# Mixer of a two-layer model: the eighth chunk's intra product goes to the state product's bank, and the second conv tile's first steps go ahead of output-weight splits

## The chip, the cores and the metric

One core of a Trainium2 chip runs the whole program. The metric is the time of one execution on the device in microseconds (us), the median over several executions. The core has a matrix engine (PE, with its weight loads shown apart as PEld), a vector engine (DVE), an activation engine (ACT), a GpSimd engine (POOL) and a queue that only starts transfers (SP). Each works through its own list in order; they meet only at semaphores. PE writes into PSUM, which has eight banks of 128 x 512 floats.

## The reference

The program computes `x = x + f(layernorm(x))` four times on a 1024 x 512 matrix: a state-space mixer, a gated feed-forward with 4-bit weights, a small attention over heads, and a feed-forward with routed low-rank parts. Only the first, the mixer, is touched:

```
proj = x_norm @ in_proj_w.T             # gate 4096, conv channels 4096+1024+1024, dt 64
xBC  = silu(conv4(proj_hbc))            # causal, 4 taps along time
x, B, C = split(xBC);  dt = softplus(dt + dt_bias);  dA = exp(-dt * exp(A_log))
state = state * dA_t + (dt*x)_t * B_t   # per head (64 heads, 8 groups), over 1024 steps
y_t   = state . C_t ;  y = y + x * D
yn    = y * rsqrt(mean(y*y over the group) + eps) * norm_weight * silu(gate)
out   = yn @ out_proj_w.T               # added to x
```

## The kernel before

The mixer runs over 8 groups `g` (8 heads, 512 channels each) and in each over 8 chunks `c` of 128 time steps; `n = 8*g + c`. Group 0 and group 7 are written out, groups 1 to 6 are one hardware loop (five jumps back). All matrix products with 512 columns on weights are made in three passes from a high and a low part (`three_pass`, L69 to 89). A group's input weights are 10 tiles (6 conv tiles and 4 of the gate), its output weights 4 tiles (numbers 10 to 13). A weight tile is loaded by SP into a ring of four, ACT makes the high part (`w_round`, L434 and L437), DVE or POOL the low part (`w_rest`, L595 and L597 on DVE, L408 on POOL): this is a split.

The scan is written in chunk form. In each chunk PE does, in this order (L868 to L930): transposes of x into bank `p_x` (L878); the transposes of the z of the chunk before into `p_in` (L838); B transposed and B.C into `p_gb` (L885, L886); the decay exponents into `p_d0` and `p_d1` (L894); a conv tile for a later half (`conv_tile`, L84 and L88) or else the next chunk's gate product; the output product of the chunk before into `p_y` (`out_product`); the state read (inter product, `p_in`, L910); the new state's part (state product, `p_x`, L916; not in the eighth chunk); in chunks 0, 1, 4 and 5 a second conv tile into `p_d1`; the product inside the chunk (intra product, L927, 16 pieces of 64 columns) into `p_y`; and, where a conv tile was made, the next chunk's gate product (`p_gate`).

On DVE a chunk has: B.C masked (L653) and copied (L654), the low part of z (L579), the decays times B.C (`em`, L661), splits, a conv tile's taps (`tile_taps`, L559, L563, L567), the residual `x_res += p_y * g_rstd` (L587), which is the reader of the output product, y from the inter product (L685), the state (L692 or L695), the y sum with the intra product (L704, in chunk 0 L709), and `z = y * gate` (L713). Between the L685 and L704 steps POOL adds `x_d` to y (L391). DVE begins each group with five small copies (L640, L642). On ACT a conv tile is taken out of its bank by `tile_in` (L445), which DVE's first tap waits for (`s_cin`), and finished by `tile_silu` (L450), which waits for the taps (`s_tap`).

Two places are touched. First, the intra product of every chunk waits for the residual of the chunk before (`s_res`), as both use `p_y`; the transposes of x of a group's first chunk wait only for ACT's copy out of `p_x` in the chunk before (`s_xs`). Second, in chunk 0 of each group ACT makes the high parts of output weights 10 and 11 and then calls `tile_in` of conv tile 1, and DVE makes their low parts and then the tile's first tap; the tile's other taps come after z, and chunk 1's decay product (L894) waits until all are done, because tile 1 lies in `p_d1`.

Of the kernel before, what the change touches and what calls it, by code (L numbers as in the profile page):

```python
# [19 lines left out]
ALU = mybir.AluOpType  # L20
# [3 lines left out]
P = 128  # L24
# [4 lines left out]
NC = L // P  # L29
# [4 lines left out]
HD = 64  # L34
# [57 lines left out]
def mixer(nc, io, ctx, x_res, ident, mean_var2, rstd2, q_prep):  # L92
# [30 lines left out]
    em = sb("em", [P, 2, HG * P])  # L123
# [75 lines left out]
    def tapped(g, hf, j):  # L199

        return (g * 2 + hf) * TILES * TAPPED[0] + (g * TILES + hf * j) * (TAPPED[1] - TAPPED[0]) + j * TAPPED[0]

    def bank_of(j):

# [222 lines left out]
    @block.scalar  # L427
    def _(act):
        def w_round(g, w):

            n = g * WT + w
            act.wait_ge(s_raw[w % RAW], 16 * (g * len(range(w % RAW, WT, RAW)) + w // RAW + 1))
            if w < TILES + KT:
                act.activation(w_hi[:, w, :], w_raw[:, w % RAW, :], ACT.Copy).then_inc(s_whi, 1)  # L434
            else:
                k = w - TILES - KT
                act.activation(w_hi[:, w, :], w_raw[:, w % RAW, :], ACT.Copy, scale=norm_w[:, bass.ds(g, 1), k])\  # L437
                    .then_inc(s_whi, 1)

        def tile_in(T, g, j, bank=None):  # L440

            p = bank_of(j) if bank is None else bank
            act.wait_ge(s_prj, T + 1)
            wait(act, s_xc, T - 1)
            act.activation(conv[:, j % 2, :], p[:], ACT.Identity, bias=conv_w[:, bass.ds(g, 1), j, TAPS],  # L445
                           scale=conv_w[:, bass.ds(g, 1), j, TAPS - 1]).then_inc(s_cin, 1)

        def tile_silu(T, g, j, hf):
            act.wait_ge(s_tap, tapped(g, hf, j) + TAPPED[hf])
            act.activation(xbc[:, j, half_cols(hf)], conv[:, j % 2, :], ACT.Silu).then_inc(s_xc, 1)  # L450

        def z_round(m):
            act.wait_ge(s_zt, m + 1)
            act.activation(zt_hi[:].rearrange("p k t -> p (k t)"), p_in[:], ACT.Copy).then_inc(s_zhi, 1)  # L454

        def gate_silu(m):

            act.wait_ge(s_gate, m + 1)
            wait(act, s_z, m)
            act.activation(gate[:], p_gate[:], ACT.Silu).then_inc(s_sg, 1)  # L460

        def group(g, last):
            for c in range(NC):
                n = g * NC + c
                first = isinstance(g, int) and n == 0
                left, now, later = conv_tiles(g, last, c)
                splits = () if last else SPLIT_IN.get(c, ())
                for tile in left:
                    tile_silu(*tile)
                act.wait_ge(s_xt, n + 1)  # L470
                wait(act, s_xd, n - 1)
                act.activation(xs[:, c % 2, :], p_x[:], ACT.Copy).then_inc(s_xs, 1)  # L472
                if not first:
                    z_round(n - 1)
                act.wait_ge(s_d, n + 1)
                wait(act, s_intra, n - 1)
                for k, p in enumerate((p_d0, p_d1)):
                    act.activation(em[:, c % 2, k * 512:(k + 1) * 512], p[:], ACT.Exp).then_inc(s_e, 1)  # L478
                for T, tg, j, _ in now:
                    tile_in(T, tg, j)  # L480
                if c == NC - 1 and not last:
                    act.wait_ge(s_gate, n + 1)
                for w in splits:
                    w_round(g + 1, w)
                for tile in now:
                    tile_silu(*tile)
                if c == 0:
                    wait(act, s_out, n)
                    w_round(g, TILES + KT)
                    w_round(g, TILES + KT + 1)  # L490
                for T, tg, j, _ in later:
                    tile_in(T, tg, j)
                act.wait_ge(s_y, n + 1)
                wait(act, s_ss, n)
                wait(act, s_v, n - 1)
                act.activation(junk[:], y[:, c % 2, :], ACT.Square, accum_out=ss[:, c % 2:c % 2 + 1])\  # L496
                    .then_inc(s_ss, 1)
                if not (last and c == NC - 1):
                    gate_silu(n + 1)
                if c == 0:  # L500
                    w_round(g, TILES + KT + 2)
                    w_round(g, TILES + KT + 3)


        for c in range(NC):
            act.wait_ge(ln_tr, c + 1)
            act.activation(xn_hi[:, :, c * P:(c + 1) * P], (p_x, p_in)[c % 2][:].rearrange("p (k t) -> p k t", k=KT),
                           ACT.Copy).then_inc(ln_hi, 1)
            if c >= CH:
                w_round(0, c - CH)  # L510
        act.wait_ge(s_const, 16 * 6)

        act.wait_ge(dt_ve, 4)
        act.activation(t_e, t_v, ACT.Abs).then_inc(dt_ac, 1)
        act.wait_ge(dt_ac, 1)
        act.activation(t_e, t_e, ACT.Exp, scale=-1.0).then_inc(dt_ac, 1)
        act.activation(head_c[:, 3:4], head_c[:, 1:2], ACT.Exp).then_inc(dt_ac, 1)
        act.wait_ge(dt_ve, 5)
        act.activation(t_r, t_w, ACT.Ln).then_inc(dt_ac, 1)
        act.wait_ge(dt_ac, 4)  # L520
        act.activation(t_rem, t_r, ACT.Exp, scale=-1.0).then_inc(dt_ac, 1)
        w_round(0, 4)
        w_round(0, 5)
        tile_in(0, 0, 0, p_tile)
        tile_in(1, 0, 1, p_d1)
        for w in range(TILES, TILES + KT):
            w_round(0, w)

        act.wait_ge(dt_tp, 4)
        act.activation(by_half(ecum_t), transposed(p_y), ACT.Exp).then_inc(dt_ac, 1)  # L530
        act.activation(by_half(dtw_t), transposed(p_gb), ACT.Exp).then_inc(dt_ac, 1)
        act.activation(by_half(etot_t), transposed(p_d0), ACT.Exp).then_inc(dt_ac, 1)
        for j in range(TILES):
            tile_silu(j, 0, j, 0)
            if j + 2 < TILES:
                tile_in(j + 2, 0, j + 2, (p_tile, p_d1)[j % 2])
        gate_silu(0)
        group(0, False)
        with act.Fori(1, G - 1) as g:
            group(g, False)  # L540
        group(G - 1, True)
        z_round(LAST)

    @block.vector
    def _(ve):
# [89 lines left out]
        def group(g, last):  # L635
# [7 lines left out]
            for c in range(NC):  # L643
# [43 lines left out]
                if c < NC - 1:  # L687
                    ve.wait_ge(s_stn, st + 1)
                    wait(ve, s_stu, st)
                    if c > 0:  # L690
                        ve.wait_ge(s_std, g * (NC - 2) + c)
                        ve.tensor_tensor(state[:], p_x[:], state_dec[:], ALU.add).then_inc(s_stu, 1)  # L692
                    else:
                        wait(ve, s_inter, st)
                        ve.tensor_copy(state[:], p_x[:]).then_inc(s_stu, 1)  # L695
                if c == 0:
                    w_rest(g, TILES + KT)
                    w_rest(g, TILES + KT + 1)
                for tile in later:
                    tile_taps(*tile, range(1))  # L700
                ve.wait_ge(s_intra, n + 1)
                if c > 0:
                    ve.wait_ge(s_txd, st)
                    ve.tensor_tensor(y[:, c % 2, :], y[:, c % 2, :], p_y[:], ALU.add).then_inc(s_y, 1)  # L704
                else:
                    ve.wait_ge(s_xd, n + 1)
                    wait(ve, s_ss, n - 1)
                    wait(ve, s_z, n - 1)
                    ve.tensor_tensor(y[:, c % 2, :], x_d[:], p_y[:], ALU.add).then_inc(s_y, 1)  # L709
# [109 lines left out]
    def _(pe):  # L819
# [36 lines left out]
                gate_product(n + 1, 0)  # L856

        def out_product(m):
            pe.wait_ge(s_zhi, m + 1)
            three_pass(pe, p_y[:], lambda k: (zt_hi[:, k, :], zt_lo[:, k, :]),  # L860
                       lambda k: (w_hi[:, TILES + KT + k, :], w_lo[:, TILES + KT + k, :]), GW // P,
                       lambda: pe.wait_ge(s_zlo, m + 1)).then_inc(s_out, 1)

        def group(g, last):
            for c in range(NC):
# [7 lines left out]
                if c > 0:  # L873
                    pe.wait_ge(s_stu, g * (NC - 1) + c)
                else:
                    wait(pe, s_xs, n)
                for j in range(GW // P):
                    mm = pe.transpose(p_x[:, j * P:(j + 1) * P], xbc[:, j, cs], ident[:])  # L878
                mm.then_inc(s_xt, 1)
# [42 lines left out]

                pe.wait_ge(s_m, 2 * (n + 1))
                pe.wait_ge(s_xdt, n + 1)
                wait(pe, s_res, n)
                for h in range(HG):
                    mm = pe.matmul(p_y[:, h * HD:(h + 1) * HD], em[:, c % 2, h * P:(h + 1) * P],  # L927
                                   x_dt[:, h * HD:(h + 1) * HD], start=True, stop=True)
                mm.then_inc(s_intra, 1)
                if now:  # L930
# [974 lines left out]
```

## Time and profile before

| | |
|---|---|
| median of 3 runs | 1380.57 us (1378.35 to 1381.72) |
| profiled execution, its own time | 1378.48 us |
| its span | 1376.7 us |
| PE busy | 1287.1 us (93%) |
| PE weight loads | 1008.3 us (73%) |
| DVE busy | 922.1 us (67%) |
| ACT busy | 676.4 us (49%) |
| POOL busy | 548.9 us (40%) |
| mean granted PE clock | 0.975 |

The profiled execution's time is 2.09 us below the median of the runs; its span is 1.8 us below its own time. The mixer's groups lie between about 66 and 1018 us of the span, and a middle group takes 119.4 us (one group's eighth intra product starts at 537.95 us, the next one's at 657.35 us). Timeline rows give the start and the busy time in us, then engine, line, operation, output and inputs, how many instructions are merged, and in brackets how long the engine sat idle before and what ended that. Ends of PE's instructions are modelled, so starts are the better measure.

### The profile page before, as it was taken

How to read it: one execution, taken by the hardware profiler on the slowest of the kernel's cores; microseconds unless marked ns; L12 is line 12 of the kernel's file. 1: busy time of each engine (PE TensorE's matmuls, PEld its weight loads, DVE VectorE, ACT ScalarE, POOL GpSimd, SP SyncE). 2: the span in 40 equal slices, each digit the busy share in tenths (PEclk: the TensorE clock that was granted, in tenths of full speed). 3: DMA queues.
4: the chain of work that ended last, by engine and by line, in shares of the span. 5: the costliest groups of instructions: out<-in, count | busy, mean ns of one | idle time of the engine just before them, and what ended most of it. 6: DMA issues, size and time to landing. Idle time of an engine off the chain costs nothing. (4 is left out here: it accounts for less than half of the span.)

```text
span 1376.7 us, 20683 instructions
## 1 busy us (share of the span) xinstructions
PE 1287.1 (93%) x6252; PEld 1008.3 (73%) x6262; DVE 922.1 (67%) x1756; ACT 676.4 (49%) x1055; POOL 548.9 (40%) x551
## 2 busy tenths in 40 slices
PE   5699999999999999999999999999869999879986
PEld 4577877877887887788788778778646766667764
DVE  5876677667667766766766676676656445368995
ACT  3465565566556556656655566655323223222220
POOL 2145345444533534443454354334333333333331
PEclk9899999999999999999999999999979999999997
DMA  4111011011102101100200120000013222131200
GB/s 150 59 48 33 1 56 40 17 32 47 31 1 63 31 16 32 55 23 1 71 23 16 32 62 16 3 30 2 8 42 115 85 76 80 50 99 29 58 16 23
DMA packets 44248, 57.61 MB, mean 42 GB/s; under 512 B 10182, under 2 KB 21156, under 8 KB 43922
## 3 DMA queue, kind: packets, MB, share of 16 engines
q1 hardware_dynamic: 44178, 56.84, 13.7%
q8 instruction: 23, 0.38, 0.1%
q14 instruction: 47, 0.39, 0.1%
HBM read 49.87 MB, written 6.96 MB: 41 GB/s over the span
## 5 line engine op out<-in xcount | busy, mean ns | idle before, releaser
L372 POOL TENSOR_TENSOR x_w<-xs,head_g 128x512 f32<-128x512 f32 x56 | 58.6, 1046 | 279.1 <-ACT xs L472 254.5
L559 DVE SCALAR_TENSOR_TENSOR conv<-p_tile,conv_taps,conv 128x511 f32<-128x511 f32 x189 | 140.9, 745 | 32.5 <-ACT conv L445 22.8
L927 PEld LDWEIGHTS p_y<-x_dt,em 128*128 128x128 f32 x1024 | 123.5, 192 | 32.9 <-issue 29.8
L391 POOL TENSOR_TENSOR y<-y,x_d 128x512 f32<-128x512 f32 x56 | 72.0, 1285 | 160.8 <-DVE y L685 160.8
L927 PE MATMUL p_y<-x_dt,em 128*128 128x64 f32 x1024 | 121.8, 272 | 11.4 <-DVE x_res L587 11.4
L661 DVE TENSOR_TENSOR em<-em,p_gb 128x512 f32<-128x512 f32 x128 | 82.2, 684 | 73.6 <-ACT em L478 73.6
L450 ACT ACTIVATE xbc<-conv 128x512 f32<-128x512 f32 x96 | 60.4, 630 | 130.1 <-DVE conv L567 73.6
L84 PE MATMUL p_tile<-xn_hi,w_hi 128*128 128x512 f32 x252 | 111.5, 443 | 2.9 <-DVE halo L563 2.9
L496 ACT ACTIVATE junk<-y 128x512 f32<-128x512 f32 x64 | 40.6, 635 | 142.3 <-DVE y L704 128.7
L559 DVE SCALAR_TENSOR_TENSOR conv<-p_d,conv_taps,conv 128x511 f32<-128x511 f32 (+2 forms) x99 | 73.8, 746 | 54.6 <-ACT conv L445 50.7
L84 PE MATMUL p_gate<-w_hi,xn_hi 128*128 128x512 f32 x256 | 106.2, 415 | 1.1 <-ACT gate L460 1.1
L408 POOL TENSOR_TENSOR w_lo<-w_raw,w_hi 128x512 fp32r<-128x512 f32 x64 | 83.1, 1314 | 59.1 <-ACT w_hi L434 59.1
L84 PE MATMUL p_y<-w_hi,zt_hi 128*128 128x512 f32 x256 | 102.5, 400 | 2.2 <-ACT zt_hi L454 2.2
L84 PE MATMUL p_y<-w_lo,zt_hi 128*128 128x512 f32 x256 | 102.4, 400 | 0.0
L84 PE MATMUL p_gate<-w_lo,xn_hi 128*128 128x512 f32 x256 | 100.3, 392 | 0.0
L84 PE MATMUL p_tile<-xn_lo,w_hi 128*128 128x512 f32 x252 | 99.3, 394 | 0.0
L478 ACT ACT_TABLE_LOAD x64 | 82.1, 1283 | 1.1
L375 POOL TENSOR_TENSOR x_dt<-xs,head_g 128x512 f32<-128x512 f32 x64 | 66.9, 1046 | 30.4 <-ACT xs L472 30.4
L450 ACT ACT_TABLE_LOAD x61 | 78.3, 1283 | 1.1
L88 PE MATMUL p_y<-w_hi,zt_lo 128*128 128x512 f32 x256 | 70.8, 399 | 0.0
L478 ACT ACTIVATE em<-p_d 128x512 f32<-128x512 f32 x128 | 69.6, 596 | 0.7
L1102 POOL TENSOR_TENSOR f_w_lo<-wf,f_w_hi 128x512 fp32r<-128x512 f32 x22 | 30.3, 1377 | 99.4 <-ACT f_w_hi L1143 99.4
(293 smaller groups left out, 3279.2 us busy)
## 6 DMA issues: line engine op xcount, KB each, us to landing
w_raw<-w SPq DMA_DIRECT2D x112, 256.0 KB, 2.8
q_words<-q SPq DMA_DIRECT2D x33, 256.0 KB, 2.7
h_ring<-h_lo_rows SPq DMA_DIRECT2D x6, 704.0 KB, 5.0
h_lo_rows<-h_rest SPq DMA_DIRECT2D x11, 256.0 KB, 2.0
x_res<-x SPq DMA_DIRECT2D x8, 256.0 KB, 4.6
out<-out_t SPq DMA_DIRECT2D x8, 256.0 KB, 2.2
h_lo_rows<-h_rest SPq DMA_DIRECT2D x11, 128.0 KB, 1.9
decay_lhs<-cum_parts SPq DMA_DIRECT2D x64, 6.0 KB
```

The source lines that it names most:

```text
L84: pe.matmul(out, lhs(k)[0], rhs(k)[n], start=(start and k == 0 and n == 0), stop=False)
L88: last = pe.matmul(out, lhs(k)[1], rhs(k)[0], start=False, stop=(k == k_tiles - 1))
L372: pool.tensor_tensor(by_head(x_w[:]), by_head(xs[:, c % 2, :]), heads(DTW, c), ALU.mult)\
L375: pool.tensor_tensor(by_head(x_dt[:]), by_head(xs[:, c % 2, :]), heads(DT, c), ALU.mult)\
L391: pool.tensor_tensor(y[:, c % 2, :], y[:, c % 2, :], x_d[:], ALU.add).then_inc(s_txd, 1)
L408: pool.tensor_tensor(w_lo[:, w, :], w_raw[:, w % RAW, :], w_hi[:, w, :].bitcast(F32), ALU.subtract)\
L450: act.activation(xbc[:, j, half_cols(hf)], conv[:, j % 2, :], ACT.Silu).then_inc(s_xc, 1)
L478: act.activation(em[:, c % 2, k * 512:(k + 1) * 512], p[:], ACT.Exp).then_inc(s_e, 1)
L496: act.activation(junk[:], y[:, c % 2, :], ACT.Square, accum_out=ss[:, c % 2:c % 2 + 1])\
L559: ve.scalar_tensor_tensor(out=conv[:, s, sh:], in0=p[:, 0:HALF - sh], scalar=conv_w[:, bass.ds(g, 1), j, tap], in1=conv[:, s, sh:], op0=AL ...
L661: ve.tensor_tensor(m, m, gm.unsqueeze(1).broadcast_to([P, HG // 2, P]), ALU.mult)\
L927: mm = pe.matmul(p_y[:, h * HD:(h + 1) * HD], em[:, c % 2, h * P:(h + 1) * P], x_dt[:, h * HD:(h + 1) * HD], start=True, stop=True)
```

## The change

The eighth chunk's intra product is written to `p_x` instead of `p_y`, and read from there by the y sum. It then waits for the chunk's own copy out of `p_x` (`s_xs`) and no longer for the residual. That wait is put ahead of each output product, and the first x transposes of a group wait for the y sum (`s_y`) of the chunk before. In chunk 0 `tile_in` and the first tap of conv tile 1 are written ahead of the splits of output weights 10 and 11, on ACT and on DVE.

```diff
+    def y_bank(c):
+        return p_x if c == NC - 1 else p_y
 # ACT, in group
+                for T, tg, j, _ in later:
+                    tile_in(T, tg, j)
                 if c == 0:
                     wait(act, s_out, n)
                     w_round(g, TILES + KT)
                     w_round(g, TILES + KT + 1)
-                for T, tg, j, _ in later:
-                    tile_in(T, tg, j)
                 act.wait_ge(s_y, n + 1)
 # DVE, in group
+                for tile in later:
+                    tile_taps(*tile, range(1))
                 if c == 0:
                     w_rest(g, TILES + KT)
                     w_rest(g, TILES + KT + 1)
-                for tile in later:
-                    tile_taps(*tile, range(1))
                 ve.wait_ge(s_intra, n + 1)
                 if c > 0:
                     ve.wait_ge(s_txd, st)
-                    ve.tensor_tensor(y[:, c % 2, :], y[:, c % 2, :], p_y[:], ALU.add).then_inc(s_y, 1)
+                    ve.tensor_tensor(y[:, c % 2, :], y[:, c % 2, :], y_bank(c)[:], ALU.add).then_inc(s_y, 1)
 # PE
         def out_product(m):
+            wait(pe, s_res, m)
             pe.wait_ge(s_zhi, m + 1)
 ...
                 if c > 0:
                     pe.wait_ge(s_stu, g * (NC - 1) + c)
                 else:
-                    wait(pe, s_xs, n)
+                    wait(pe, s_y, n)
 ...
-                wait(pe, s_res, n)
+                if c < NC - 1:
+                    wait(pe, s_res, n)
+                else:
+                    pe.wait_ge(s_xs, n + 1)
                 for h in range(HG):
-                    mm = pe.matmul(p_y[:, h * HD:(h + 1) * HD], em[:, c % 2, h * P:(h + 1) * P],
+                    mm = pe.matmul(y_bank(c)[:, h * HD:(h + 1) * HD], em[:, c % 2, h * P:(h + 1) * P],
                                    x_dt[:, h * HD:(h + 1) * HD], start=True, stop=True)
```

## Rows read from the trace of the kernel before

**Rows 1.** Waits, all engines: engine, line, releaser: us in total, times, longest us.

```profile
PE p_y L927 <- DVE x_res L587: 11.4, 9, 1.5
```

**Rows 2.** Groups by line: busy us, mean ns, idle before and its releaser.

```profile
L894 PE MATMUL p_d<-decay_rhs,decay_lhs 90*128 90x512 bf16 x128 | 38.3, 380 | 3.7 <-DVE conv L567 3.6
```

**Rows 3.** Windows: one middle group's eighth chunk; length, busy us by engine, PE clock.

```profile
530.04:543.06 13.02, 11.52 (x59) 9.13 (x59) 8.23 (x14) 8.16 (x13) 5.97 (x6) 1.00 0.25 83
```

**Rows 4.** Timeline of PE from a middle group's eighth intra product on.

```profile
537.95 1.97 PE L927 MATMUL p_y<-x_dt,em 128*128 128x64 f32 x16 [1.50 <-DVE x_res L587]
...
542.57 0.60 PE L878 MATMUL p_x<-identity,xbc 128*128 128x128 f32 x4
543.00 0.60 PE L838 MATMUL p_in<-identity,z 128*128 128x128 f32 x4
```

**Rows 5.** Timeline of DVE over the same group boundary.

```profile
540.83 0.69 DVE L704 TENSOR_TENSOR y<-y,p_y 128x512 f32<-128x512 f32 x1 [1.47 <-POOL y L391]
541.55 0.69 DVE L713 TENSOR_TENSOR z<-y,gate 128x512 f32<-128x512 f32 x1
544.68 0.20 DVE L640 TENSOR_SCALAR head_g<-dt_t 128x64 f32 x1 [2.44 <-issue]
...
546.46 1.28 DVE L661 TENSOR_TENSOR em<-em,p_gb 128x512 f32<-128x512 f32 x2
548.56 0.75 DVE L559 SCALAR_TENSOR_TENSOR conv<-p_tile,conv_taps,conv 128x511 f32<-128x511 f32 x1 [0.82 <-ACT conv L445]
```

**Rows 6.** Timeline of POOL in the eighth chunk and in the first chunk after.

```profile
535.38 2.57 POOL L408 TENSOR_TENSOR w_lo<-w_raw,w_hi 128x512 fp32r<-128x512 f32 x2 [3.22 <-ACT w_hi L434]
...
553.04 1.05 POOL L365 TENSOR_TENSOR state_dec<-state,head_g 128x512 f32<-128x512 f32 x1 [3.91 <-DVE state L695]
```

**Rows 7.** Timeline of PE, first chunk's second conv tile to the second chunk's decays.

```profile
552.44 1.07 PE L88 MATMUL p_d<-xn_hi,w_lo 128*128 128x512 f32 x4
553.35 1.89 PE L927 MATMUL p_y<-x_dt,em 128*128 128x64 f32 x16
...
559.65 0.61 PE L894 MATMUL p_d<-decay_rhs,decay_lhs 90*128 90x512 bf16 x2 [0.38 <-DVE conv L567]
```

**Rows 8.** Timeline of ACT in the same first chunk.

```profile
552.87 1.32 ACT L437 ACTIVATE w_hi<-w_raw,norm_scale 128x512 fp32r<-128x512 f32 x2
554.09 0.76 ACT L445 ACTIVATE conv<-p_d,conv_taps 128x512 f32<-128x512 f32 x1
```

**Rows 9.** Timeline of DVE in the same first chunk.

```profile
553.73 1.56 DVE L597 SCALAR_TENSOR_TENSOR w_lo<-w_raw,norm_scale,w_hi 128x512 fp32r<-128x512 f32 x2 [0.77 <-ACT w_hi L437]
555.22 0.74 DVE L559 SCALAR_TENSOR_TENSOR conv<-p_d,conv_taps,conv 128x511 f32<-128x511 f32 x1
555.88 0.67 DVE L709 TENSOR_TENSOR y<-x_d,p_y 128x512 f32<-128x512 f32 x1
...
558.86 0.73 DVE L567 SCALAR_TENSOR_TENSOR conv<-halo,conv_taps,conv 128x3 f32<-128x3 f32 x3
559.58 1.42 DVE L597 SCALAR_TENSOR_TENSOR w_lo<-w_raw,norm_scale,w_hi 128x512 fp32r<-128x512 f32 x2
```

**Rows 10.** Timeline, chunk 4: a conv tile passed on without splits between.

```profile
493.08 1.07 PE L88 MATMUL p_d<-xn_hi,w_lo 128*128 128x512 f32 x4
...
494.34 0.78 ACT L445 ACTIVATE conv<-p_d,conv_taps 128x512 f32<-128x512 f32 x1 [2.16 <-PE p_d L88]
495.35 0.75 DVE L559 SCALAR_TENSOR_TENSOR conv<-p_d,conv_taps,conv 128x511 f32<-128x511 f32 x1 [2.53 <-ACT conv L445]
```

**Rows 11.** Timeline of ACT and of DVE in group 0's first chunk.

```profile
75.69 1.32 ACT L437 ACTIVATE w_hi<-w_raw,norm_scale 128x512 fp32r<-128x512 f32 x2
...
78.64 0.67 DVE L709 TENSOR_TENSOR y<-x_d,p_y 128x512 f32<-128x512 f32 x1
```

**Rows 12.** Timeline of POOL and of DVE in the mixer's very last chunk.

```profile
1006.12 1.27 POOL L391 TENSOR_TENSOR y<-y,x_d 128x512 f32<-128x512 f32 x1 [3.32 <-DVE y L685]
...
1007.60 0.69 DVE L704 TENSOR_TENSOR y<-y,p_y 128x512 f32<-128x512 f32 x1 [1.55 <-PE p_y L927]
```

## The prediction

> **What bounds the kernel.** I read the waits first. Of everything that PE waits for inside the mixer's groups, two places belong to this change. The intra product (L927) waits for the residual 9 times, 11.4 us in all [rows 1]: once near the end of each of the eight groups, 1.25 us in group 0, 1.5 in each of groups 1 to 6, 0.96 in group 7, and once 0.16. The decay products (L894) wait for conv taps for 3.6 us in all [rows 2]: 1.31 in group 0 and about 0.38 in each of groups 1 to 6. Then the windows: in a middle group's eighth chunk PE is busy 11.52 of 13.02 us at full granted clock, and the 1.50 that are missing are that one wait [rows 3, 4]. So in the groups PE is the bound, with two holes per group (119.4 us), and the time of the mixer is PE's work plus those holes. Everything below asks how large each hole is afterwards, in one middle group (the one whose rows are shown); the rest of PE's list moves rigidly with it, and nothing later in a group has slack to give back or to absorb, since PE shows no other hole there.
>
> **Edit 1, the bank of the eighth intra product.** Removed: the wait for the residual, 1.50 us; the intra product would start 1.5 earlier, and its other conditions (em, x_dt, the copy out of p_x) are fulfilled long before. The gate product follows; it wants POOL's low parts of the gate weights, done at 535.38 + 2.57 = 537.95 [rows 6], while it could start at about 538.1: no hold. The x transposes after it would start at 542.57 - 1.5 = 541.07 [rows 4].
>
> What is late next: they now wait for the y sum (s_y). DVE's y sum starts at 540.83, released by POOL's add and not by the intra product, so it does not get earlier; it ends at 541.52 [rows 5]. From DVE's end to PE's start takes 0.06: the last tap ends at 558.86 + 0.73 = 559.59 and L894 starts at 559.65 [rows 9, 7]. So x transposes at 541.58. Behind the waiting transposes stand PE's z transposes, then the next group's whole list; for the x transposes wait ACT's copy and POOL's x_w, and as they come 1.0 earlier than before even so, those lose nothing. The z transposes come 0.43 after them (543.00 - 542.57), at 542.01, but z itself ends at 541.55 + 0.69 = 542.24 [rows 5], again unmoved: z transposes at 542.30. Before they were at 543.00. The hole of 1.50 therefore turns into one of about 0.8 further on, and the gain is 0.70. I take 0.05 off for a restart after idling: 0.65.
>
> Does it last? In the five jumps back DVE sits 2.44 us before its first small copy ("issue") after z, and z does not move, so DVE's chain stays where it is: em done at 546.46 + 1.28 = 547.74, then the first conv tap, which was at 548.56 because of ACT's tile_in [rows 5] and is asked for at 548.56 - 0.65 = 547.91. There is 0.17 left, so DVE doesn't bind. Seven boundaries: 7 x 0.65 = 4.5 us.
>
> Group 7 has no boundary behind it. There the y sum starts at 1007.60, released by PE, while POOL's add is done at 1006.12 + 1.27 = 1007.39 [rows 12]. Hardly anything to win: 0.1 us. The bounds for one boundary are 0 (below) and 1.5 (the whole hole); 0.65 stands on rows.
>
> The wait added ahead of each output product is for a residual of one chunk earlier, fulfilled long before. Whether a further fulfilled wait costs PE time: L927 stands behind three waits, and starts 0.91 after the four L88 products before it, which is four times 0.23, their pace [rows 7]. So it costs nothing; the bounds are 0 and, at 0.05 for each of some 60, 3 us.
>
> **Edit 2, the first chunk.** Before, in the middle group: ACT makes the two high parts from 552.87 on and tile_in at 554.09 [rows 8]; DVE makes the low parts from 553.73, the first tap at 555.22, the y sum at 555.88 [rows 9]. Both splits lay in time in which PE was still at the conv tile, so ACT and DVE would have idled.
>
> After: tile_in can start when PE has done the tile. In chunk 4, with nothing between, ACT starts 494.34 - 493.08 = 1.26 after the last four products start, and DVE's tap 1.01 after ACT [rows 10]. The last four start at 552.44 [rows 7], so ACT at 553.70 and the tap at 554.71: 0.51 earlier than 555.22. But the splits come behind: ACT's high parts start at about 554.40; the first low part was 0.86 after the first high part (553.73 - 552.87), so it is ready at 555.26, and the tap frees DVE after 0.66 (555.88 - 555.22) at 555.37. Two low parts without a wait take 1.42, 0.08 less to the next start [rows 9]: 1.34. The y sum comes at 556.71 to 556.75 instead of 555.88: later by 0.85; I take 0.87. The intra product, which it also waits for, is over by 553.35 + 1.89 = 555.24, so before and after the y sum waits for DVE's own list. Behind the y sum stand z, the other taps and the splits 12 and 13, with nothing that they could skip; the last tap ends at 560.46 and L894 starts at 560.52 instead of 559.65. PE's hole grows from 0.38 to about 1.25. The z transposes ahead of it do not matter, as L894 waits for the later taps anyway. ACT's silu of tile 1, the copies behind it and SP's loads of the next weights, which wait for splits 12 and 13, move by at most the same 0.87, as PE does. In sum, an idle stretch that was filled is now empty, and its work stands between the intra product and the taps.
>
> Group 0 is another case. ACT's high parts start at 75.69, behind tile 0's silu and not behind an early end of anything on PE [rows 11]. tile_in takes that place, the tap comes 1.01 later at 76.70, 0.66 + 1.34 on the y sum at 78.70, against 78.64: 0.06. Group 7 I count like a middle group. Sum: 7 x 0.87 + 0.06 = 6.1 us later.
>
> The bounds per group: if both splits were still hidden the tap's 0.51 would remain and the hole of 0.38 would close (-0.4); if tile_in's start takes 0.15 longer, or high part 11 holds DVE, +1.1.
>
> A rule of the Trainium skill bears on that. In the rows the first pair of low parts takes 1.56 and the later pair 1.42, and POOL's state_dec runs from 553.04 to 554.09, over the start of the first pair [rows 6, 9]. The page "SBUF — State Buffer", section "SBUF: two separate sides", says that GpSimd and a vector instruction with two SBUF inputs hold one pair of ports exclusively, the loser waiting in full. By that rule the moved pair, which starts after 554.09, takes 1.42, as I have put it; by a pair that always needed 1.56 the delay would be 1.0 per group and the sum 1 us more.
>
> **Sum.** -4.5 - 0.1 + 6.1 = +1.5 us. Against the profiled execution: span 1376.7 to 1378.2, own time 1378.48 to 1380.0. That execution was 2.09 below the median, so the median goes from 1380.57 to 1382.1.
>
> **Rivals.**
> A, the earlier first tap shortens the chain to L894: tile 1's taps end earlier and L894's wait goes, -3.6 us [rows 2], and with edit 1's 4.6 the time is 1372.4. For it: the tap is 0.5 earlier. Against: the splits are the same 1.3 us of DVE and now have no cover.
> B, edit 1 gives its whole hole, 7 x 1.5 = 10.5, less 6.1: 1376.2. That wants z 0.8 us earlier; its chain runs over POOL's add and DVE's list, none of which waits for the intra product.
> C, on the other side: the boundary gives nothing, and the splits' 6.1 remain: 1386.7. Place: the start of each group in the loop. If DVE's gap after z, 2.44 us here, depends on what PE does, or if the restart of PE behind two real waits in a row takes longer, DVE's chain of 3.06 us to the end of em (544.68 to 547.74) becomes the bound. It begins to eat at a gap of 2.6 and has eaten all at 3.3; from 0.3 of gain left per boundary downward the total passes 0.3%. For it: only 0.17 of slack. Against: the gap was measured with the same code.
> D, the edits cost beside this: the extra waits show with up to 3 us, or splits 12 and 13 now meet POOL's x_w: up to 1385, inside the range.
>
> **Chances.** Forecast 0.74 (own range 1379.5 to 1384.5), A 0.07, B 0.05, C 0.10, D 0.04. The range for 8 in 10 reaches from 1377.5, towards B, to 1386.5, towards C. A measurement here can't tell less than about 0.3% (4.1 us) from no change. A and part of B are faster by more: 0.11. C and a little of D are slower by more: 0.14. The rest, 0.75, is within.
>
> **What would show it.** Right: L927 in chunk 8 without idle; at the boundary the z transposes idle about 0.2 to 0.7 behind z, the x transposes about 0.5 behind y; a period of 119.4 + 0.2; DVE idle 1.7 before the first tap of tile 1, the y sum at once behind low part 11; L894's idle 1.25 in groups 1 to 7. Wrong: if L894's idle is 0.4 or less (A), if z transposes don't wait (B), if the taps of tile 0 follow em without idle time (C).

## The result and the profile after

| kernel | median us (lowest to highest, runs) | kernel before, beside it |
|---|---|---|
| changed kernel | 1382.88 (1380.26 to 1386.07, 20) | 1379.07 (1377.46 to 1384.91, 20) |

The ratio is 1.0021, with a 95% interval of 1.0013 to 1.003: 2.9 us slower, 1.8 to 4.1. Here and below, a difference in us without further words is this ratio, less one, times the median of the kernel before; the two medians themselves lie 3.8 apart. The 2.9 are inside the 0.3% that I had called no change, but clear of zero. I had forecast +1.5 us, and 1382.1. The absolute time came out only 0.8 off, and that is luck: the median of three runs from which I started, 1380.57, was 1.5 above the one of twenty runs, and this hid as much of an error of 2.3 in the difference of the medians. The profiled execution has a span of 1379.2 us, against 1376.7.

First the waits of PE over the mixer in the changed kernel (columns as in [rows 1]):

```profile
PE p_d L899 <- DVE conv L571: 10.0, 8, 1.3
PE p_in L842 <- DVE z L717: 5.9, 5, 2.5
PE p_x L883 <- DVE y L708: 3.6, 7, 0.6
```

L899 was L894, L842 was L838, L883 was L878. The 11.4 us behind the residual [rows 1] are gone down to one wait of 0.2; the new 3.6 at the x transposes stand at seven boundaries; and the decay products wait 10.0 instead of 3.6 [rows 2]. The 5.9 for z are a wait of 0.16 in group 0 and four in the last group, the longest of them, 2.5, at the z of the last chunk, which was 1.5 before. Then PE's timeline of the same middle group (start, busy time, operation, idle time before):

```profile
538.33 1.89 PE L935 MATMUL p_x<-x_dt,em 128*128 128x64 f32 x16
...
543.61 0.66 PE L883 MATMUL p_x<-identity,xbc 128*128 128x128 f32 x4 [0.55 <-DVE y L708]
544.34 0.66 PE L842 MATMUL p_in<-identity,z 128*128 128x128 f32 x4
...
553.83 1.07 PE L88 MATMUL p_d<-xn_hi,w_lo 128*128 128x512 f32 x4
554.74 1.89 PE L935 MATMUL p_y<-x_dt,em 128*128 128x64 f32 x16
...
561.96 0.60 PE L899 MATMUL p_d<-decay_rhs,decay_lhs 90*128 90x512 bf16 x2 [1.30 <-DVE conv L571]
```

The eighth intra product (L935) now has no idle time [rows 4], and the second hole has grown from 0.38 [rows 7] to 1.30. DVE over the same stretch:

```profile
542.87 0.69 DVE L708 TENSOR_TENSOR y<-y,p_x 128x512 f32<-128x512 f32 x1 [1.47 <-POOL y L395]
543.59 0.69 DVE L717 TENSOR_TENSOR z<-y,gate 128x512 f32<-128x512 f32 x1
546.96 0.20 DVE L644 TENSOR_SCALAR head_g<-dt_t 128x64 f32 x1 [2.67 <-issue]
...
548.74 1.27 DVE L665 TENSOR_TENSOR em<-em,p_gb 128x512 f32<-128x512 f32 x2
549.95 0.75 DVE L563 SCALAR_TENSOR_TENSOR conv<-p_tile,conv_taps,conv 128x511 f32<-128x511 f32 x1
...
556.19 0.75 DVE L563 SCALAR_TENSOR_TENSOR conv<-p_d,conv_taps,conv 128x511 f32<-128x511 f32 x1 [1.84 <-ACT conv L449]
556.86 1.41 DVE L601 SCALAR_TENSOR_TENSOR w_lo<-w_raw,norm_scale,w_hi 128x512 fp32r<-128x512 f32 x2
558.18 0.68 DVE L713 TENSOR_TENSOR y<-x_d,p_y 128x512 f32<-128x512 f32 x1
...
561.17 0.73 DVE L571 SCALAR_TENSOR_TENSOR conv<-halo,conv_taps,conv 128x3 f32<-128x3 f32 x3
```

and ACT and POOL in the first chunk:

```profile
555.08 0.78 ACT L449 ACTIVATE conv<-p_d,conv_taps 128x512 f32<-128x512 f32 x1 [0.73 <-PE p_d L88]
555.75 1.32 ACT L441 ACTIVATE w_hi<-w_raw,norm_scale 128x512 fp32r<-128x512 f32 x2
```

```profile
554.42 1.04 POOL L369 TENSOR_TENSOR state_dec<-state,head_g 128x512 f32<-128x512 f32 x1 [3.03 <-DVE state L699]
```

**Where the 2.9 us are.** I count from chunk to chunk on PE, by the start of the decay products of chunk 1. In the middle groups before they come at 320.83, 440.25, 559.65, a period of 119.40; after at 322.63, 442.29, 561.96, a period of 119.67. So a group costs 0.27 more, where I had 0.22: +0.92 in chunk 1 (the hole, 1.30 for 0.38) and -0.66 at the boundary. From group 0's first B transpose to these products of group 6 it is 731.00 us in the trace of before and 732.38 after (798.45 - 67.45; 801.29 - 68.91): +1.4. Further executions, told of below, give 731.02 and 731.03 for before and 732.38, 732.41 and 732.43 for after, so this much is the edits, and it is firm. What lies ahead of the first B transpose belongs to no edit and varies (67.45, 68.08, 67.72 before; 68.91, 68.80, 67.67, 68.71 after). The rest arises behind it: from the first B transpose to the first product of the next phase before has 952.36, 952.52 and 952.25, after 953.58, 954.69, 954.08 and 956.33, and the mean is 2.3 longer (954.67 against 952.38). Of this later. The 0.6 that are left of 2.9 (2.9 - 2.3) lie within the interval.

### The profile page after: what moved, and what is told of

Read it like the earlier page. It is cut to its first block and busy times, and to the rows that moved or that the text cites. A ratio compares the mean times of both kernels' runs of the same rounds, so it can differ in the third digit from the quotient of the medians.

```text
span 1379.2 us, 20756 instructions
## 1 busy us (share of the span) xinstructions
PE 1289.3 (93%) x6262; PEld 1008.8 (73%) x6262; DVE 919.9 (67%) x1756; ACT 677.7 (49%) x1055; POOL 549.0 (40%) x551
## 5 line engine op out<-in xcount | busy, mean ns | idle before, releaser
L935 PEld LDWEIGHTS p_y<-x_dt,em 128*128 128x128 f32 x896 | 108.6, 192 | 15.3 <-issue 12.2
L935 PE MATMUL p_y<-x_dt,em 128*128 128x64 f32 x896 | 106.1, 271 | 0.2 <-DVE x_res L591 0.2
```

The costliest lines, as they stand in the source:

```text
L935: mm = pe.matmul(y_bank(c)[:, h * HD:(h + 1) * HD], em[:, c % 2, h * P:(h + 1) * P], x_dt[:, h * HD:(h + 1) * HD], start=True, stop=True)
```

## The experiments

Each kernel was timed beside the kernel before, on the same chip. There were two sets: each edit alone, the splits last and the wait alone (kernel before: 1379.14, 23 runs), and the rest (1379.39, 23 runs).

### Each edit alone

**Edit 1 alone.** The changed kernel with the order of before on ACT and DVE:

```diff
+                if c == 0:
+                    wait(act, s_out, n)
+                    w_round(g, TILES + KT)
+                    w_round(g, TILES + KT + 1)
                 for T, tg, j, _ in later:
                     tile_in(T, tg, j)
...
+                if c == 0:
+                    w_rest(g, TILES + KT)
+                    w_rest(g, TILES + KT + 1)
                 for tile in later:
                     tile_taps(*tile, range(1))
```

> The kernel before with the bank edit alone (eighth intra product in p_x, its waits), ACT's and DVE's order in the first chunk as before. Theory of the prediction: each of seven group boundaries wins 0.65 us, bound by z, the tail 0.1, so 4.6 us less than before; the hole before the decay products of chunk 1 stays at 0.38 (1.31 in group 0). Rival C: the boundary wins nothing, time as before. Rival B: the whole hole of 1.5 us goes, 10.5 us less.

Measured: 1375.22, ratio 0.9966 [0.9951, 0.9981], 4.7 us faster; I had 4.6. The period is 118.73, which is 0.67 less. Its waits:

```profile
PE p_x L883 <- DVE y L708: 3.7, 7, 0.6
PE p_d L899 <- DVE conv L571: 3.5, 7, 1.3
```

A wait of 1.50 was taken away, and 0.67 of it was gained.

**Edit 2 alone.** The kernel before with the order of the changed kernel:

```diff
                 for T, tg, j, _ in later:
                     tile_in(T, tg, j)
                 if c == 0:
                     wait(act, s_out, n)
                     w_round(g, TILES + KT)
                     w_round(g, TILES + KT + 1)
...
                 for tile in later:
                     tile_taps(*tile, range(1))
                 if c == 0:
                     w_rest(g, TILES + KT)
                     w_rest(g, TILES + KT + 1)
```

> The kernel before with the reordering alone (tile_in and first tap of conv tile 1 ahead of splits 10 and 11 on ACT and DVE). Theory of the prediction: the splits lose the cover of the conv tile; the decay products of chunk 1 wait 0.87 to 0.92 us longer in groups 1 to 6 and about as much in group 7, nothing in group 0: 6 us more than before. Rival A: the earlier tap closes the hole of 0.38 per group, 3.6 us less.

Measured: 1391.66, ratio 1.0077 [1.0058, 1.0097], 10.6 us slower, against 6.1. So the edits do not add: -4.7 and +10.6 make +5.9, together they cost 2.9. The list of waits explains only the forecast part, 6.4 us more at L894 (10.0 for 3.6):

```profile
PE p_y L927 <- DVE x_res L587: 10.4, 8, 1.5
PE p_d L894 <- DVE conv L567: 10.0, 8, 1.3
```

The starts of L894 show it: 202.07, 322.40, 444.31, 564.63, 686.55, 806.90, 928.35. The steps are 119.9 into group 1 and then 120.3 (119.40 + 0.93, as forecast) and, every second time, 121.9, or 121.45 into group 7. Windows of this kernel (length, busy time of PE, PEld, DVE, ACT, POOL, granted clock, DMA share, GB/s), at the boundary into group 2, which was not lengthened, and at the one into group 3, which was:

```profile
299.00:302.00 3.00, 2.23 (x18) 2.23 (x19) 2.13 (x4) 0.63 (x1) 1.51 (x2) 1.00 0.87 280
...
420.00:424.00 4.00, 3.90 (x21) 3.55 (x22) 2.46 (x5) 0.95 (x2) 1.36 (x2) 0.70 0.47 165
424.00:426.00 2.00, 2.00 (x8) 1.64 (x7) 0.37 (x1) 0.41 (x2) 0.00 (x0) 0.74 0.01 4
```

and PE at the second:

```profile
420.10 2.27 PE L927 MATMUL p_y<-x_dt,em 128*128 128x64 f32 x16 [1.50 <-DVE x_res L587]
422.13 0.78 PE L84 MATMUL p_gate<-w_hi,xn_hi 128*128 128x512 f32 x1
```

PE stood idle for 1.50 us, and in the next microseconds the granted clock was 0.70 and 0.74 on the mean, between the upper level of 2.4 GHz and the lower of 1.2. The intra product took 2.27 us where it takes 1.97 [rows 4]. Each such place costs 1.6 us. The three long steps make 4.7 us, and 6.1 + 4.7 is 10.8: the trace has the same 10.8 up to the decay products of group 7 (860.94 from the first B transpose, for 850.16), and 10.6 are measured. In the kernel before the same idle of 1.50 is there in the same groups, and its clock over 418 to 422 us is 1.00. With edit 1 the 1.50 is gone, and the clock stays up at these places. So edit 1 is worth more beside edit 2 than alone: 7.7 us (10.6 - 2.9) for 4.7 by the measured times, 9.3 for 4.8 in the traces up to group 7. I had no rival for this.

Why the clock falls here and not in the kernel before is not shown. What is new is the hole of 1.30 in each group, but it does not stand beside the fall: the last one before it is 98 us earlier (322.40) and the next comes only at 443. It also changes when the boundaries come, every 120.3 us and no longer every 119.40. No run that keeps the 1.50 has the one without the other.

### Is the added wait ahead of the output products free?

```diff
         def out_product(m):
+            wait(pe, s_res, m)
             pe.wait_ge(s_zhi, m + 1)
```

> The kernel before with nothing but the wait for the residual of one chunk earlier added ahead of each output product (63 waits that are always fulfilled). Theory of the prediction: 0 us. Rival D: a fulfilled wait costs PE up to 0.05 us each, 3 us more, which would be the part of the measured 2.9 us that the groups' rows do not show.

Measured, the kernel before with that line alone: 1379.81, ratio 0.9999 [0.9984, 1.0015], and a period of 119.40 as in the kernel before. Free, as forecast; the 3 us of rival D are refuted.

### What bounds the boundary, y or z?

Edit 1 alone, but the eighth intra product in `p_d1`, so that the x transposes needn't wait for the y sum:

```diff
     def y_bank(c):
-        return p_x if c == NC - 1 else p_y
+        return p_d1 if c == NC - 1 else p_y
...
-                    wait(pe, s_y, n)
+                    wait(pe, s_xs, n)
```

> As e1_bank_only, but the eighth intra product goes to the bank p_d1, so the x transposes of the next group wait for nothing of the y sum (as in the kernel before). Theory: the hole at the boundary is set by z, which the z transposes need, and the wait of the x transposes costs nothing by itself: period as in e1_bank_only, 118.74 us, with PE's idle now all before the z transposes. Rival: the new wait for the y sum is what is left of the hole; without it 0.55 us less per boundary, 3.8 us in all.

Measured: 1376.79, ratio 0.9975 [0.9962, 0.9988], 3.4 us faster, and the same period as with edit 1 alone (118.73 to 118.78 for 118.72 to 118.74). PE's timeline shows the whole remainder in front of the z transposes:

```profile
539.39 0.60 PE L883 MATMUL p_x<-identity,xbc 128*128 128x128 f32 x4
540.82 0.66 PE L842 MATMUL p_in<-identity,z 128*128 128x128 f32 x4 [0.83 <-DVE z L717]
```

The two kernels were timed in different sets; their intervals overlap, and the periods are equal. So the wait for y in edit 1 costs nothing of its own; z is what the boundary waits for, as I had worked out.

### What the moved splits cost, and where they fit

**Splits last.** The changed kernel with the two low parts behind the tile's taps:

```diff
                 for tile in later:
                     tile_taps(*tile, range(1))
-                if c == 0:
-                    w_rest(g, TILES + KT)
-                    w_rest(g, TILES + KT + 1)
...
                 if c == 0:
+                    w_rest(g, TILES + KT)
+                    w_rest(g, TILES + KT + 1)
                     w_rest(g, TILES + KT + 2)
                     w_rest(g, TILES + KT + 3)
```

> The changed kernel, but DVE's low parts of output weights 10 and 11 moved behind all taps of conv tile 1, in front of those of 12 and 13. Theory: what costs in the reordering is the place of the two low parts between first tap and y sum, not the early tile_in; without them the y sum comes 0.5 us earlier than in the kernel before, the hole ahead of the decay products closes in groups 1 to 7 and mostly in group 0 (together 4.8 us), beside the 4.6 of the bank: 9.4 us less than before. Rival: four low parts in a row make DVE late in chunk 1 (output product waits for low part 13, or em comes late) and the hole only moves: about as e1_bank_only, 4.6 less, or worse.

Measured: 1374.13, ratio 0.9948 [0.993, 0.9967], 7.2 us faster than before. From DVE and from PE:

```profile
554.92 3.53 DVE L601 SCALAR_TENSOR_TENSOR w_lo<-w_raw,norm_scale,w_hi 128x512 fp32r<-128x512 f32 x4
```

The fourth of these low parts by itself, and POOL beside it:

```profile
556.91 1.53 DVE L601 SCALAR_TENSOR_TENSOR w_lo<-w_raw,norm_scale,w_hi 128x512 fp32r<-128x512 f32 x1
```

```profile
556.73 1.17 POOL L376 TENSOR_TENSOR x_w<-xs,head_g 128x512 f32<-128x512 f32 x1 [6.89 <-ACT xs L476]
```

```profile
554.97 0.61 PE L898 MATMUL p_d<-decay_rhs,decay_lhs 90*128 90x512 bf16 x2
...
557.25 1.07 PE L88 MATMUL p_tile<-xn_hi,w_lo 128*128 128x512 f32 x4
558.50 0.50 PE L84 MATMUL p_y<-w_hi,zt_hi 128*128 128x512 f32 x1 [0.18 <-DVE w_lo L601]
```

The decay products have no idle time in any group but the first (0.37, for 1.31 before). The splits are therefore the whole of what holds L894, and the sooner tap is worth nothing beside them. But the period is 118.77, not the 118.4 that the closed hole should give: the fourth low part now ends at 558.45, and the output product behind it starts at 558.50, where the four products before it, 0.91 after their start, would have let it start at 558.16. A hole of 0.38 was closed and one of 0.34 opened; PE's row shows only 0.18 of it as idle, and the other 0.08 of the period I can't place. The fourth low part is late not because four are too many: it takes 1.53 where the others take 0.75, as it starts behind POOL's `x_w` (556.73 to 557.90). With 0.75 it would have ended at 557.7, ahead of 558.16. In group 7 the fourth one starts ahead of POOL, all four take 2.73, and it is POOL's `x_w` that takes 1.45. Beyond edit 1's 4.6 this kernel gains 1.5 in group 0 (13.45 us from the first B transpose to the decay products, for 14.94); the 1.1 that are left of the 7.2 I can't place, and the interval is some 2.6 wide to either side. Of my 9.4 the part that failed is the hole that only moved, which was the rival.

**One split early, one late.** On ACT and DVE split 10 goes ahead of the tile's first steps; ACT makes high part 11 behind `tile_in`, DVE its low part at the end:

```diff
                 if c == 0:
                     w_rest(g, TILES + KT)
-                    w_rest(g, TILES + KT + 1)
                 for tile in later:
                     tile_taps(*tile, range(1))
...
                 if c == 0:
+                    w_rest(g, TILES + KT + 1)
                     w_rest(g, TILES + KT + 2)
                     w_rest(g, TILES + KT + 3)
```

> The changed kernel with split 10 back ahead of tile_in and first tap, and split 11 behind: high part after tile_in on ACT, low part behind all taps on DVE. In e3_splits_last the hole before the decay products closed, but PE then waited 0.18 (0.5 by the period, 118.75) for low part 13 before the output product of chunk 1. Theory: DVE idles 1.8 us before the first tap, room for one low part; with one less behind the taps low part 13 is no longer late: period about 118.2 us, 9 us less than before in all. Rival: split 10 still delays tile_in or the tap on ACT or DVE, or low part 13 stays late: as e3_splits_last, 7 less.

Measured: 1372.70, ratio 0.9941 [0.9922, 0.9959], 8.1 us faster; I had 9. The period is 118.35 (437.66 to 556.01): 0.67 less by edit 1 and 0.38 less by the hole. 7 x 1.05 and 0.7 in group 0 make the 8.1. DVE shows why it fits: one split fills the idle time ahead of the tap, and three at the end are done at 558.01.

```profile
550.48 0.90 DVE L602 SCALAR_TENSOR_TENSOR w_lo<-w_raw,norm_scale,w_hi 128x512 fp32r<-128x512 f32 x1 [0.77 <-ACT w_hi L441]
551.57 0.75 DVE L564 SCALAR_TENSOR_TENSOR conv<-p_d,conv_taps,conv 128x511 f32<-128x511 f32 x1 [0.19 <-issue]
...
555.94 2.07 DVE L602 SCALAR_TENSOR_TENSOR w_lo<-w_raw,norm_scale,w_hi 128x512 fp32r<-128x512 f32 x3
```

**And y's first step ahead of the residual.** What is left is z. POOL's add waits for DVE's L685 step, which stands behind the residual and a tap. In the eighth chunk the residual needn't come first any more, since the intra product no longer waits for it:

```diff
+                def y_inter():
+                    ...
+                if c == NC - 1:
+                    y_inter()
                 if not first:
                     residual(n - 1, (c - 1) % NC)
                 for tile in now:
                     tile_taps(*tile, range(2, TAPPED[tile[3]]))
-                if c > 0:
-                    ...
+                if 0 < c < NC - 1:
+                    y_inter()
```

> As e6_one_early, and in the eighth chunk DVE forms y from the inter product ahead of the residual and the last taps instead of behind them (it could not pay before, as PE waited for the residual there). Theory: what is left of the hole at the boundary (0.55 idle before the x transposes, 0.3 before the z transposes) is z's lateness; POOL's add starts about 0.8 earlier (it is held until its low part 9 is done), y sum and z about 1.4 earlier, the hole closes: 0.85 us less per boundary and 0.6 in the last chunk than e6_one_early, together 6.5 us, period about 117.4. Rival: PE's gate product waits for POOL's low part 9, or DVE after its jump back binds: half of that or nothing.

Measured: 1366.46 (1363.63 to 1367.28, 5 runs), ratio 0.9892 [0.987, 0.9915], 14.9 us faster than the kernel before, and so faster than both the kernel before and the changed one. The period is 117.30 (418.73 to 536.03, and 536.03 to 653.33). DVE at the boundary:

```profile
531.03 0.68 DVE L685 TENSOR_TENSOR y<-p_in,head_g 128x512 f32<-128x512 f32 x1
531.63 0.74 DVE L592 SCALAR_TENSOR_TENSOR x_res<-p_y,g_rstd,x_res 128x512 f32<-128x512 f32 x1
...
533.27 0.69 DVE L711 TENSOR_TENSOR y<-y,p_x 128x512 f32<-128x512 f32 x1
533.99 0.69 DVE L720 TENSOR_TENSOR z<-y,gate 128x512 f32<-128x512 f32 x1
```

and PE:

```profile
534.83 0.60 PE L887 MATMUL p_x<-identity,xbc 128*128 128x128 f32 x4
535.26 0.60 PE L846 MATMUL p_in<-identity,z 128*128 128x128 f32 x4
```

z ends at 534.68 and is there before PE asks. One window over nearly all eight groups shows that hardly anything is left to gain from waits in this stretch (length, then PE's busy time first, the granted clock near the end):

```profile
83.00:957.00 874.00, 873.45 (x4440) 701.41 (x4438) 601.75 (x1173) 528.21 (x811) 393.81 (x388) 1.00 0.11 31
```

PE is busy for 873.45 of 874.00 us. Outside it a wait of 1.2 for the decay products of group 0 is left, and the last group's waits for z. 7 x (119.40 - 117.30) is 14.7, and 0.7 in group 0 makes 15.4, for 14.9 measured.

### The rest of the difference: the changed and the old kernel again

> The changed kernel once more, beside the others on one chip. Both edits together were 2.9 us slower than before, while its groups' rows give 1.2 and 1.5 lay ahead of the first group, where PE's clock rose later. Theory: the part ahead of the groups differs from one execution to the next, so this one's groups again have a period of 119.67 us (0.27 more than before) and the part ahead of the groups need not be longer. Rival: the part ahead of the first group is longer by 1.5 us each time the changed program runs.

Measured: 1383.85 (12 runs), ratio 1.0017 [1.0001, 1.0033], 2.3 us slower than the kernel before.

> The kernel before, unchanged, for the time ahead of its first group (start of the first B transpose, 67.45 us in its first profile; 68.91 and 68.80 in two profiles of the changed kernel, 66.99 to 69.44 in kernels with other edits behind it). Theory: that time differs from execution to execution with the transfers at the start and the moment at which PE's clock rises, so this one may lie anywhere from 67 to 69.5; the period of a middle group is 119.4 us again. Rival: it is 67.4 with this program each time, and the changed program is 1.4 us late each time.

> As before_b: theory 67 to 69.5 us ahead of the first group, rival 67.4.

> The changed kernel again, for the same time ahead of the first group. Theory: anywhere from 67 to 69.5 us, period 119.67. Rival: 68.8 to 68.9 again.

> As after_c: theory 67 to 69.5 us ahead of the first group, rival 68.8 to 68.9.

Four single executions: 1379.42 and 1378.46 for the kernel before, 1382.09 and 1383.87 for the changed one. The period is 119.4 and 119.67 again. The first profile of the changed kernel has its first B transpose at 68.91 instead of 67.45, ahead of anything that was changed. That the change brings this each time is refuted by the execution of 1382.09, which has 67.67. The last group does show a difference. Windows over its last chunks, of the first profiled execution of the changed kernel, then of the one of 1382.09 and of the one profiled beside the median of 1383.85, and last of the kernel before with the added wait alone:

```profile
975.00:990.00 15.00, 12.85 (x68) 9.53 (x67) 8.17 (x17) 8.19 (x13) 5.87 (x7) 1.00 0.00 1
```

```profile
975.00:990.00 15.00, 12.90 (x58) 9.72 (x59) 7.72 (x16) 6.63 (x11) 5.84 (x6) 0.89 0.00 1
```

```profile
990.00:1005.00 15.00, 12.32 (x57) 9.27 (x56) 9.09 (x26) 6.60 (x11) 5.49 (x6) 0.90 0.08 11
```

```profile
975.00:990.00 15.00, 13.94 (x65) 10.83 (x64) 8.53 (x17) 8.16 (x13) 8.07 (x10) 0.89 0.00 0
```

In that order the three of the changed kernel reach the next phase 953.58, 954.08 and 954.69 us after the first B transpose. The fourth, 1383.87, has 0.89 in the first window and 0.97 in the second, and 956.33. The three of the kernel before have 1.00 in both windows and 952.25 to 952.52. No edit touches the instructions of chunks 4 to 6; with no weights of a next group to multiply, PE waits there for z (1.06 at a time) and for the gate. Three of four traces with the change show the clock lower here. Of the four without it one does too, the one with the added wait alone, and it still reaches the next phase after 952.47 us, as the kernel before does. So a lower clock in this stretch doesn't need the change, and has no fixed price.

By chunks: at the B transposes of the eighth chunk the changed kernel is 1.4 behind the kernel before where the clock had stayed up (932.25 us after the first B transpose, for 930.80 to 930.89), and 2.5 to 3.0 behind in the other three; the added wait alone is 0.3 behind. From there to the next phase the kernel before takes 21.4 to 21.7, the changed one 20.2 to 22.5. The mean of some 0.9 us beyond the 1.4 (2.3 - 1.4) may come from where the clock falls, but it isn't shown: no run moved only these chunks, and the traces of the kernel before are of three of its faster executions (1378.46 to 1379.42, where single ones went up to 1387.15).

## Why the prediction held, step by step

**The bound.** PE, its list rigid, two holes per group: right. The windows and the constant 119.67 show it, and the last experiment confirms it by closing both.

**Edit 1.** The x transposes start 0.05 after the end of the y sum (543.56, 543.61), the z transposes 0.06 after z (544.28, 544.34); I had 0.06 for both. A hole of 1.50 became one of 0.85: 0.55 ahead of the x transposes and 0.30 ahead of the z transposes, which start 0.73 after them and not 0.43. I had 0.8. (The row of the z transposes shows no idle time, since the modelled end of the x transposes reaches up to it; my sign "if z transposes don't wait" had to be read from the starts.) The gain is 0.66 to 0.67 per boundary for my 0.65, and 4.7 us for 4.6 alone. The last chunk behaves as forecast too: its intra product comes without a wait, and its y sum is now released by POOL [rows 12], about 0.1 sooner.

**Slack of 0.17 before DVE binds.** In this group it is used up: the gap behind z is 2.67 instead of 2.44 [rows 5], and the first tap of tile 0 follows em without idle time, which I had named as the sign of rival C. That isn't the change's doing. I had read one jump back of five, and the shortest: in the kernel before they take 2.44 to 2.66, in the changed one 2.44 to 2.72. A gap of 2.6, at which I had put the start of rival C, was there already. But nothing came of it, as no product of PE waits for that tap soon enough. The sign was badly chosen; the period was the right one.

**Edit 2.** ACT's `tile_in` comes 1.25 after the last four products (I had 1.26), the tap 1.11 after that (1.01, from chunk 4, was 0.1 too short), the y sum 1.99 after the tap (2.00). It comes 4.35 after the last four products for 3.44 before [rows 7, 9]: +0.91, and +0.92 at L899, in place of +0.87. DVE waits 1.84 before the tap (forecast 1.7), and L899 1.30 (1.25). Group 7 is not like a middle group: L899 waits 0.85 there, and the group is later by 0.73 and not 0.87 (its step of 119.23 for 119.16, with the 0.66 of the boundary added).

**Group 0.** Forecast +0.06, measured -0.16 (83.69 - 68.91 against 82.39 - 67.45). These are rows of group 0 in the changed kernel, of ACT and of DVE:

```profile
77.15 0.76 ACT L449 ACTIVATE conv<-p_d,conv_taps 128x512 f32<-128x512 f32 x1
```

```profile
77.94 0.75 DVE L563 SCALAR_TENSOR_TENSOR conv<-p_d,conv_taps,conv 128x511 f32<-128x511 f32 x1 [0.76 <-ACT conv L449]
78.61 1.40 DVE L601 SCALAR_TENSOR_TENSOR w_lo<-w_raw,norm_scale,w_hi 128x512 fp32r<-128x512 f32 x2
79.93 0.68 DVE L713 TENSOR_TENSOR y<-x_d,p_y 128x512 f32<-128x512 f32 x1
```

Everything ahead is 1.46 later than before (68.91 - 67.45). So `tile_in` starts at 75.69 in the old count, just as forecast, and the y sum comes 1.99 after the tap (2.00). The tap, though, comes 0.79 after `tile_in`, where I had put the 1.01 of chunk 4: that is the whole 0.22. The step from ACT to DVE, which I took for a constant, was 0.79 here, 1.01 in chunk 4 and 1.11 in a middle group.

**The pair of low parts.** In a middle group the moved pair takes 1.41, and POOL's state_dec, 554.42 to 555.46, is over before it begins at 556.86: the pair that overlapped it took 1.56 [rows 6, 9]. The rule of the Trainium skill ("SBUF — State Buffer", "SBUF: two separate sides"), that such a vector instruction and GpSimd exclude each other from a pair of ports, gave just this; a pair that always needs 1.56 is excluded by the row.

**The sum.** The two edits came to +1.4 us up to group 6 and +1.5 up to group 7 (851.61 - 850.16), against +1.5. That it is so near is partly luck. Edit 2's 6.1 are three errors that cancel: six middle groups at 0.92 for 0.87 (0.3 more), group 0 at -0.16 for +0.06 (0.2 less) and group 7 at 0.73 for 0.87 (0.1 less). The 1.4 us between this and the measured 2.9 arise behind these rows, or are noise; the interval begins at 1.8. A term that I had at nothing is the granted clock. In the changed kernel it may stand for some 0.9 us, which isn't shown; without edit 1 it costs 4.7, and my working for edit 2 would have been wrong by 4.5 us for that edit alone.

A and B are refuted: the hole before the decays did not close, and the boundary did not give its whole 1.5. So is C, as the boundary gave 0.66. Of D the extra wait cost nothing, and splits 12 and 13, 561.89 to 563.31, are almost over when POOL's `x_w` starts at 563.13.

## What to carry to other kernels

When a wait is taken away, work out the end of the next operand in line before counting the gain: here only 0.66 of 1.50 was gained, and the operand that mattered (z) had to be brought forward by another edit, the order of two DVE steps, worth 6.8 us (14.9 - 8.1), more than edit 1. A step between two engines, or a gap, that is read once is no constant; read it in several groups. Work that lies in an idle stretch is free only there; before moving it, give each of its pieces its own place (one split early, one late closed the hole; both early left 0.38 of it, both late moved it), and look at what the other engines do at the new place: four low parts were late because one of them met POOL. A hole can cost more than its length (1.50 us of idle time cost 1.6 more at three boundaries with edit 2 alone), so two edits that change idle times should be timed alone and together.

## What the runs showed of the hardware

**The clock after short holes.** In the kernel with edit 2 alone the granted clock fell at the idle stretch of 1.50 us, to a mean of 0.70 over 4 us and 0.74 over the next 2, and 1.6 us were lost; over 422 to 424 us it was 0.50, the lower level. It did so at three of six such boundaries, every second one, with the same instructions at all six. In the four traces with the same 1.50 but a hole of 0.38 in place of 1.30, and a period of 119.4 in place of 120.3, it did so at none of 24. In the last group the place of the fall changed from one execution to the next. The Trainium skill ("TensorE: Matmul & The Clock Gate", "Part 1: The HAM clock gate") says that the chip judges PE's activity in windows that run on by themselves, so that one kernel meets them at changing places. The alternation and the changing places agree with it. No run here varied the length of a hole alone or the period alone, and I draw no threshold from this.

**A loop's jump back.** On DVE the first instruction of a group behind a jump came 2.44 to 2.81 us after the last one of the group before, without any wait shown ("issue"). In none of the kernels did PE wait for it.

**Two SBUF inputs on DVE beside POOL.** The same pair of low parts took 1.56 to 1.62 us where it began over POOL's instruction, and 1.40 to 1.42 alone. One low part that began 0.18 behind POOL's `x_w` took 1.53 us for 0.75, 0.78 more, with 0.99 of `x_w` still to run; where it began first, it was `x_w` that took longer, 1.45 for 1.04 to 1.08.
